# Channel attention: extremes of keys by a chain of maxima, one row of exponentials added on VectorE, inverses by logarithm and one Newton step

## The chip, the cores and the metric

The kernel runs on one core of a Trainium2 chip, as one program. The time is the core's own, in microseconds; three runs were made of the kernel before. One more execution was profiled.

## The reference

Four layers act on x of shape (4, 256, 64, 64) in float32, each as x + layer(group_norm(x)): a windowed attention, a linear attention, a channel attention over 7 x 7 windows, and a dynamic convolution. The change touches the third:

```python
q = jnp.einsum('bchw,oc->bohw', x, w_q)
kmap = jnp.einsum('bchw,oc->bohw', x_pad, w_k)
vmap = jnp.einsum('bchw,oc->bohw', x_pad, w_v)
...
kwin = jnp.concatenate([kwin[:, :half] + rel_h, kwin[:, half:] + rel_w], axis=1)
...
attn = jax.nn.softmax(q[..., None] * kwin, axis=-1)
out = jnp.sum(attn * vwin, axis=-1)
```

Each channel of each pixel has a softmax of its own over its 49 neighbours: the score is q times (key + bias), where the bias depends on the window's row in the first 128 channels and on its column in the other 128. So per pixel and channel there are 49 exponentials, a sum of them, a sum of them times the values, and one division.

## The kernel before

The function `channel_attention` works on bands of 16 image rows (`NB` = 16 of them, 4 images x 4). A band has four tiles of 128 channels x 512 pixels (8 rows): half h (channels) = 0, 0, 1, 1 and part u = 0, 1, 0, 1. Below, a tile with u = 0 is called even, with u = 1 odd. There are 64 tiles in all. A tile has 49 steps j, one for each tap: seven rows o of seven taps i. All five engines walk through (band, tile, step) in their own loops, written out for one band and repeated by a hardware loop; what stands in which step is set by small tables of step numbers (`PROJ_AT`, `NEAR`, `EXT_AT`, `INVERT_AT`, `DIVIDE_AT`, `BACK_AT`, `ADD_AT`), and semaphores with counts join the engines.

A step of each engine:

- VectorE, `multiply` (L1795): (key + bias) x query into one of three banks of PSUM, `stage`. It waits until the exponential three steps back has read that bank.
- TensorE, `shift` (L1545): a product with minus the identity takes from the same bank the largest score `top`. Then `add_up` (L1552): four transposes of 128 x 128 add the map of exponentials of two steps back to `pe_sum`, and four more the weighted map of twelve steps back to `pv_sum`. The order in a step is weighted map, shift, exponentials.
- ScalarE, `exponential` (L1671): the exponential of the bank into `se`, which has four buffers of seven taps each (a row).
- GpSimd, `weigh` (L1705): four or three taps of exponentials times the values, into `ev`. Two of these make a row of seven, 14 a tile.

Beside that, in the tables' steps:

- The largest score is found ahead, for the half that comes next. `near_step_of` (VectorE) takes the maximum and the minimum over four keys, along a row of the image or down a column, depending on the half: L1742 makes that of two neighbours (`pair`), and L1752, a `tensor_reduce` over a pattern of 2 x 2 elements of `pair` at distances 3 and 2, makes that of seven in a row (`near`). Keys come in four parts, `near` in two pieces for each part and extreme: 8 pairs and 16 reductions for a half, all in steps 4 to 33 of the even tile. `extreme_step` then goes over the seven windows (L1769, L1771) and multiplies by the query (L1778, L1780): 34 operations for a half, 10 in the even tile from step 34 on and 24 in the odd one. Below they are called extremes.
- `project` (TensorE, L1534) makes the next half's keys, queries and values in the bank `pj`, in ten parts of two steps each; ScalarE copies each part out (L1645), two steps after it was begun. Before the next part may be written the bank has to be copied. Even tiles have six parts (keys and queries), odd ones four (values).
- The division of tile t-1 falls into tile t: ScalarE copies `pe_sum` to `es` in step 1 (L1659, `take_e_sums`), VectorE inverts it in four pieces in steps 3, 5, 7 and 9 (L1803), multiplies in step 12 (L1811), TensorE turns the result back in step 20 and VectorE adds it to x in step 23 (L1819).

The buffers `se` are freed for the row four rows later by two conditions: summed on TensorE and weighed on GpSimd.

## Time and profile before

| | us |
|---|---|
| median of 3 runs | 9316.44 (9316.26 to 9318.12) |
| profiled execution | 9307.04 |
| its span | 9305.5 |
| TensorE busy | 8011.6 (86%) |
| VectorE busy | 5823.2 (63%) |
| ScalarE busy | 3539.4 (38%) |
| GpSimd busy | 4537.8 (49%) |

The channel attention runs from about 4,040 to 8,210 us of the span. PE is TensorE (PEld its weight loads), DVE VectorE, ACT ScalarE and POOL GpSimd. The digits of a slice are tenths of its time in which the engine was busy. Durations of two instructions that follow each other overlap a little, so the time that one takes from a queue is read from the distance of two starts. In brackets at the end of a timeline's row stands the idle time before it, and what ended it.

### The profile page before, as it was taken

The numbers are of one execution on the slowest core, as the hardware profiler recorded it, in microseconds if no ns is written. First come the engines' busy times: TensorE is split into PE (matmuls) and PEld (weight loads), VectorE is DVE, ScalarE is ACT, GpSimd is POOL, SyncE is SP. The second block draws the span as 40 slices with busy tenths as digits, with TensorE's granted clock in tenths as the row PEclk, the third lists the DMA queues.
The fourth block names the chain that finished last, engine by engine and source line by source line (L and its number), as shares of the span: only waits on it lengthen the run. The fifth ranks groups of instructions, "written<-read, shape, count | busy, mean of one in ns | idle before, by whom it ended". The sixth has DMA issues, their size and how long they took to land. (4 is left out here: it accounts for less than half of the span.)

```text
span 9305.5 us, 159969 instructions
## 1 busy us (share of the span) xinstructions
PE 8011.6 (86%) x55850; PEld 6805.6 (73%) x55850; DVE 5823.2 (63%) x9258; ACT 3539.4 (38%) x6969; POOL 4537.8 (49%) x2070
## 2 busy tenths in 40 slices
PE   3888886759996777569999999999999999938999
PEld 2666664649996565458888888888888888836777
DVE  3555555454442343479888989888888889842110
ACT  3444444313332222234445545444445545530000
POOL 2444443003332000047778878777777878831111
PEclk9999998879998888889999999999999999969999
DMA  5111113846775455410000000000000000052111
GB/s 195 52 52 61 53 52 129 295 143 144 146 146 142 173 160 149 159 70 17 6 17 17 17 17 17 17 13 17 6 17 17 17 17 17 8 164 105 63 61 55
DMA packets 435343, 703.76 MB, mean 76 GB/s; under 512 B 273645, under 2 KB 280301, under 8 KB 425390
## 3 DMA queue, kind: packets, MB, share of 16 engines
q1 hardware_dynamic: 389550, 502.28, 17.4%
q0 software_dynamic: 38656, 176.79, 6.3%
q10 hardware_dynamic: 6528, 16.78, 0.6%
q8 instruction: 357, 5.85, 0.3%
q14 instruction: 252, 2.06, 0.1%
HBM read 422.53 MB, written 273.22 MB: 75 GB/s over the span
## 5 line engine op out<-in xcount | busy, mean ns | idle before, releaser
L1705 POOL TENSOR_TENSOR e_ev<-e_se,e_v 128x2048 f32<-128x2048 f32 (+1 forms) x896 | 3311.6, 3714 | 916.6 <-ACT e_se L1671 916.6
L1671 ACT ACTIVATE e_se<-e_stage 128x512 f32<-128x512 f32 x3136 | 1878.2, 599 | 2082.4 <-PE e_stage L1545 2056.3
L1795 DVE SCALAR_TENSOR_TENSOR e_stage<-e_k,e_rl,e_qp 128x512 f32<-128x512 f32 x3136 | 2302.6, 746 | 318.6 <-ACT e_se L1671 279.2
L1552 PE MATMUL e_pv_sum<-e_ident,e_ev 128*128 128x128 f32 x12544 | 1874.1, 273 | 38.1 <-issue 37.6
L1552 PE MATMUL e_pe_sum<-e_ident,e_se 128*128 128x128 f32 x12544 | 1878.0, 272 | 0.1
L1552 PEld LDWEIGHTS e_pe_sum<-e_ident,e_se 128*128 128x128 f32 x12544 | 1556.3, 139 | 227.3 <-issue 2.0
L1552 PEld LDWEIGHTS e_pv_sum<-e_ident,e_ev 128*128 128x128 f32 x12544 | 1487.9, 141 | 264.8 <-issue 211.4
L1545 PE MATMUL e_stage<-e_top,e_minus 128*128 128x512 f32 x3136 | 1508.7, 481 | 45.3 <-DVE e_stage L1795 43.9
L363 POOL TENSOR_TENSOR a_pr<-a_pr,a_rden 128x480 f32<-128x480 f32 x512 | 493.9, 985 | 683.0 <-DVE a_rden L583 683.0
L852 POOL DMA_DIRECT2D agg<-c_ot x384 | 329.0, 862 | 950.9 <-DVE c_ot L910 839.1
L886 PE MATMUL c_pa<-c_x_high,c_w_high 128*128 128x320 f32 x1920 | 602.3, 314 | 111.4 <-DVE c_w_low L965 111.4
L1545 PEld LDWEIGHTS e_stage<-e_top,e_minus 128*128 128x128 f32 x3136 | 596.1, 190 | 98.3 <-DVE e_stage L1795 71.4
L1534 PE MATMUL e_pj<-e_xb,e_wt 128*128 128x385 f32 (+5 forms) x1280 | 572.8, 531 | 72.6 <-ACT e_v L1645 60.9
L548 ACT ACTIVATE a_pr<-a_ps,a_nmax 128x240 f32<-128x240 f32 x1024 | 459.0, 461 | 402.8 <-DVE a_nmax L577 402.8
L886 PE MATMUL c_pa<-c_x_high,c_w_low 128*128 128x320 f32 x1920 | 603.8, 315 | 0.0
L886 PE MATMUL c_pa<-c_x_low,c_w_high 128*128 128x320 f32 x1920 | 602.1, 314 | 0.0
L1771 DVE SCALAR_TENSOR_TENSOR e_ext<-e_near,e_rl,e_ext 128x512 f32<-128x512 f32 x768 | 575.3, 749 | 0.9
L577 DVE TENSOR_REDUCE a_nmax<-a_ps 128x2 f32<-128x480 f32 x512 | 312.1, 651 | 406.9 <-PE a_ps L441 406.9
L1752 DVE TENSOR_REDUCE e_near<-e_pair 128x192 f32<-128x768 f32 (+2 forms) x512 | 514.7, 1005 | 0.6
L2100 DVE TENSOR_TENSOR f_xr<-f_pc,f_xr 128x512 f32<-128x512 f32 x64 | 44.2, 691 | 742.6 <-PE f_pc L2013 742.6
L1967 POOL TENSOR_TENSOR f_x_low<-f_xb,f_x_high 128x1400 fp32r<-128x1400 f32 x32 | 106.3, 3326 | 796.6 <-ACT f_x_high L2043 796.6
L2013 PE MATMUL f_pc<-f_x_high,f_w_high 128*128 128x512 f32 x1152 | 467.3, 406 | 22.3 <-POOL f_x_low L1967 22.3
(154 smaller groups left out, 12357.7 us busy)
## 6 DMA issues: line engine op xcount, KB each, us to landing
xn<-n_xnp POOLq DMA_DIRECT2D x32, 2450.0 KB, 14.9
qkv<-b_ot SPq DMA_DIRECT2D x120, 512.0 KB, 5.8
c_xt<-qkv SPq DMA_DIRECT2D x384, 160.0 KB, 4.3
agg<-c_ot POOLq DMA_DIRECT2D x384, 160.0 KB, 3.0
n_xt<-x SPq DMA_DIRECT2D x24, 2048.0 KB, 11.8
a_xb<-xn SPq DMA_DIRECT2D x32, 840.0 KB, 6.2
e_xb<-xn SPq DMA_DIRECT2D x16, 1540.0 KB, 7.0
f_xb<-xn SPq DMA_DIRECT2D x32, 700.0 KB, 6.0
```

The costliest lines, as they stand in the source:

```text
L363: nc.gpsimd.tensor_tensor(w, w, by, ALU.mult).then_inc(normalised, 1)
L548: last = nc.scalar.activation(pr[P % BUF][:, i, e, :], ps[:, 2 * s + i, e * NK:(e + 1) * NK], ACT.Exp, bias=nmax[P % BUF][:, i, e:e + 1], ...
L886: last = nc.tensor.matmul(pa[:, u, b, 0:NBLK * WW].rearrange("p (k c) -> p k c", c=WW), lhsT=w[u][:, dx].rearrange("p o y -> p (o y)"), rh ...
L1534: last = nc.tensor.matmul(out, lhsT=wt[:, w, g, (h % 2) * PART:(h % 2 + 1) * PART], rhs=rhs, start=g == 0, stop=g == HALVES - 1)
L1545: nc.tensor.matmul(stage[:, bank_of(t, j), :], lhsT=minus[:], rhs=top[h][:, u * TPX:(u + 1) * TPX], start=False, stop=True, skip_group_che ...
L1552: last = nc.tensor.matmul(acc[:, c * PART:(c + 1) * PART], lhsT=src[:, c * PART:(c + 1) * PART], rhs=ident[:], is_transpose=True, start=j ...
L1671: nc.scalar.activation(se[(t * K2 + o) % NSE][:, i], stage[:, bank_of(t, j), :], ACT.Exp)\
L1705: nc.gpsimd.tensor_tensor(split(ev[(t * NG2 + g) % NEV][:, 0:size]), split(se[(t * K2 + o) % NSE][:, i:i + size]), window(v[h], h, u, o, i ...
L1752: nc.vector.tensor_reduce(to, pairs, AX.XY, op).then_inc(near_step, 1)
L1771: nc.vector.scalar_tensor_tensor(rows(ext[:]), win, r[:, o:o + 1], rows(ext[:]), ALU.add, op)\
L1795: nc.vector.scalar_tensor_tensor(rows(stage[:, bank_of(t, j), :]), win, rl[:, h, o:o + 1], rows(qp[:]), ALU.add, ALU.mult).then_inc(multip ...
L2013: last = nc.tensor.matmul(pc[:, u, m].rearrange("p (r c) -> p r c", c=WW), lhsT=w[:, g, t, m * PART:(m + 1) * PART], rhs=x[:, g, dy:dy + R ...
```

## The change

Four things are changed, all in `channel_attention`.

The extreme of seven keys is made by three elementwise operations instead of two: of two neighbours (`pair`, as before), of four (`four`, a buffer of one part), and of seven, written back into `pair`. The 2 x 2 reductions and the buffer `near` are gone; the number and the steps of the pieces stay.

The seven exponential maps of window row 3 (`SUM_ROW`) are no longer added on TensorE one by one. VectorE adds them in four pieces of 128 pixels, in steps 31, 33, 35 and 37 of the same tile, into `row_sum`, and TensorE adds that once, in step 41. Each piece is a `tensor_reduce` over seven elements that lie 512 elements (2 KB) apart.

The inverse of the sum of exponentials is no longer VectorE's reciprocal. ScalarE makes exp(-ln(es)) in step 3, GpSimd multiplies it by the sum (`check`, after its second weighing), and VectorE makes (product - 2) x estimate in step 10, which is minus the inverse after one Newton step. The addition to x becomes a subtraction.

Of the extremes, which `EXT_AT` spreads over free steps, some move by one to four steps, since other steps are free now.

```diff
-        near = [sb(f"near{i}", [PART, HPX]) for i in range(2)]
+        four = [sb(f"four{i}", [PART, 6 * PW]) for i in range(2)]
...
+        row_sum = sb("row_sum", [PART, TPX])
...
-        INVERT_AT = (3, 5, 7, 9)
-        NINV = len(INVERT_AT)
-        DIVIDE_AT, BACK_AT, ADD_AT = 12, 20, 23
+        SUM_ROW = 3
+        ROW_AT = (31, 33, 35, 37)
+        NROW = len(ROW_AT)
+        ROW_ADD_AT = 41
+        NSUM = NTAP - K2 + 1
+        LN_AT, CHECK_AFTER = 3, 1
+        INVERT_AT, DIVIDE_AT, BACK_AT, ADD_AT = 10, 12, 20, 23
...
-            + [(1, j) for j in range(NTAP - 2) if j not in (*INVERT_AT, DIVIDE_AT, ADD_AT)]
+            + [(1, j) for j in range(NTAP - 2) if j not in (INVERT_AT, DIVIDE_AT, ADD_AT, *ROW_AT)]
...
             def sum_exponential(n, t, j, first=False):
                 o, i = divmod(j, K2)
+                if o == SUM_ROW:
+                    return
...
+            def sum_row(n, t):
+                pe.wait_ge(row_summed, tiles(n, t, NROW, NROW))
+                add_up(pe_sum, row_sum, SUM_ROW * K2).then_inc(e_summed, 1)
...
+                if j == ROW_ADD_AT:
+                    sum_row(n, t)
...
+            def nearly_invert(n, t):
+                act.wait_ge(e_taken, tiles(n, t, 1, 1))
+                if later(n, t):
+
+                    act.wait_ge(divided, tiles(n, t, 1, 0))
+                nc.scalar.activation(rs[:], es[:], ACT.Ln).then_inc(near_inverse, 1)
+                act.wait_ge(near_inverse, tiles(n, t, 2, 1))
+                nc.scalar.activation(rs[:], rs[:], ACT.Exp, scale=-1.0).then_inc(near_inverse, 1)
...
+                if j == LN_AT and (t or not first):
+                    nearly_invert(n, t - 1)
...
+            def check(n, t):
+
+                pool.wait_ge(near_inverse, tiles(n, t, 2, 2))
+                nc.gpsimd.tensor_tensor(es[:], es[:], rs[:], ALU.mult).then_inc(checked, 1)
...
-                pairs = bass.AP(tensor=a.tensor, offset=a.offset,
-                                ap=[a.ap[0], [PW, tall], [1, wide], [3 * away, 2], [2 * away, 2]])
...
-                nc.vector.tensor_reduce(to, pairs, AX.XY, op).then_inc(near_step, 1)
+                high_, wide = (size, PW) if h % 2 == 0 else (HR, size)
+                of_four = four[i][:, 0:high_ * wide].rearrange("p (r c) -> p r c", c=wide)
+                if piece == 1:
+
+                    src, to, by, count_ = key_part(pair[i][:], h, c), of_four, 2, (PW, HR)[h % 2] - 3
+                else:
+                    src, to, by, count_ = of_four, key_part(pair[i][:], h, c), 3, (WW, R2)[h % 2]
...
+                nc.vector.tensor_tensor(to, a, z, op).then_inc(near_step, 1)
...
-            def invert(n, t, p):
+            def sum_row(n, t, p):
...
+                nc.vector.tensor_reduce(row_sum[:, s], se[(t * K2 + SUM_ROW) % NSE][:, :, s].rearrange("p i x -> p x i"),
+                                        AX.X, ALU.add).then_inc(row_summed, 1)
+
+            def invert(n, t):
+
+                dve.wait_ge(checked, tiles(n, t, 1, 1))
+                nc.vector.scalar_tensor_tensor(rs[:], es[:], 2.0, rs[:], ALU.subtract, ALU.mult).then_inc(inverted, 1)
```

How the order moves, at three places of the first band, which is written out. In a row stands the line, the operation, what it writes and reads, and how many follow each other. First ScalarE in the second tile (odd), from the copy of the sums on; e_se is an exponential, e_v a copy of projected values. Before:

```order
L1659 ACTIVATE e_es<-e_pe_sum 128x512
L1671 ACTIVATE e_se<-e_stage 128x512
L1645 ACTIVATE e_v<-e_pj 128x385
L1671 ACTIVATE e_se<-e_stage 128x512 x2
L1645 ACTIVATE e_v<-e_pj 128x385
```

and now:

```order
L1685 ACTIVATE e_es<-e_pe_sum 128x512
L1706 ACTIVATE e_se<-e_stage 128x512
L1671 ACTIVATE e_v<-e_pj 128x385
L1706 ACTIVATE e_se<-e_stage 128x512
L1692 ACT_TABLE_LOAD
L1692 ACTIVATE e_rs<-e_es 128x512
L1694 ACT_TABLE_LOAD
L1694 ACTIVATE e_rs<-e_rs 128x512
L1706 ACTIVATE e_se<-e_stage 128x512
L1671 ACTIVATE e_v<-e_pj 128x385
```

Between the exponentials of steps 3 and 4 stand two table loads and two activations, in this tile as in every other.

Second, VectorE in steps 31 to 38 of the same tile; e_stage is a multiply, e_ext an extreme. Before:

```order
L1795 SCALAR_TENSOR_TENSOR e_stage<-e_k,e_rl,e_qp 128x512 x2
L1769 TENSOR_SCALAR e_ext<-e_near,e_rl 128x512
L1795 SCALAR_TENSOR_TENSOR e_stage<-e_k,e_rl,e_qp 128x512
L1771 SCALAR_TENSOR_TENSOR e_ext<-e_near,e_rl,e_ext 128x512
L1795 SCALAR_TENSOR_TENSOR e_stage<-e_k,e_rl,e_qp 128x512 x2
```

and now:

```order
L1844 SCALAR_TENSOR_TENSOR e_stage<-e_k,e_rl,e_qp 128x512
L1855 TENSOR_REDUCE e_row_sum<-e_se 128x128
L1844 SCALAR_TENSOR_TENSOR e_stage<-e_k,e_rl,e_qp 128x512
L1820 SCALAR_TENSOR_TENSOR e_ext<-e_pair,e_rl,e_ext 128x512
L1844 SCALAR_TENSOR_TENSOR e_stage<-e_k,e_rl,e_qp 128x512
L1855 TENSOR_REDUCE e_row_sum<-e_se 128x128
L1844 SCALAR_TENSOR_TENSOR e_stage<-e_k,e_rl,e_qp 128x512 x2
L1855 TENSOR_REDUCE e_row_sum<-e_se 128x128
L1844 SCALAR_TENSOR_TENSOR e_stage<-e_k,e_rl,e_qp 128x512
L1820 SCALAR_TENSOR_TENSOR e_ext<-e_pair,e_rl,e_ext 128x512
L1844 SCALAR_TENSOR_TENSOR e_stage<-e_k,e_rl,e_qp 128x512
L1855 TENSOR_REDUCE e_row_sum<-e_se 128x128
```

Each of the four reductions stands behind a multiply and ahead of the next.

Third, TensorE at the start of row 3, in step 22 and after it in the first tile; e_pj is a projection. Now:

```order
L1563 MATMUL e_stage<-e_top,e_minus 128x512
L1570 MATMUL e_pe_sum<-e_ident,e_se 128x128 x4
L1570 MATMUL e_pv_sum<-e_ident,e_ev 128x128 x4
L1563 MATMUL e_stage<-e_top,e_minus 128x512
L1570 MATMUL e_pv_sum<-e_ident,e_ev 128x128 x4
L1563 MATMUL e_stage<-e_top,e_minus 128x512
L1552 MATMUL e_pj<-e_xb,e_wt 128x374
```

The row e_pe_sum is missing from the second step on, for seven steps; before, it stands in each.

## Rows read from the trace of the kernel before

**Rows 1.** The page: busy tenths of its 40 slices

```profile
PE   3888886759996777569999999999999999938999
DVE  3555555454442343479888989888888889842110
```

**Rows 2.** Busy times by tile, an even, an odd and an even tile

```profile
core 0: us, PE busy (x) PEld busy (x) DVE busy (x) ACT busy (x) POOL busy (x), PEclk, DMA share, GB/s
6009.30:6073.90 64.60, 64.32 (x470) 55.20 (x469) 60.53 (x90) 32.75 (x58) 51.62 (x15) 1.00 0.05 18
6073.90:6137.00 63.10, 60.66 (x461) 53.66 (x459) 52.58 (x78) 32.00 (x56) 52.27 (x15) 1.00 0.01 2
6137.00:6208.00 71.00, 67.40 (x468) 56.26 (x469) 65.25 (x91) 32.48 (x57) 50.87 (x15) 0.98 0.01 2
```

**Rows 3.** Waits of 2,000 us of the stage: us in total, times, longest

```profile
DVE e_stage L1795 <- ACT e_se L1671: 129.0, 213, 2.4
```

**Rows 4.** Timeline of a steady step (start us, us, engine, line)

```profile
6000.48 0.48 PE L1545 MATMUL e_stage<-e_top,e_minus 128*128 128x512 f32 x1
6000.79 0.60 PE L1552 MATMUL e_pe_sum<-e_ident,e_se 128*128 128x128 f32 x4
...
6000.99 0.60 ACT L1671 ACTIVATE e_se<-e_stage 128x512 f32<-128x512 f32 x1 [0.51 <-PE e_stage L1545]
...
6001.23 0.60 PE L1552 MATMUL e_pv_sum<-e_ident,e_ev 128*128 128x128 f32 x4
6001.58 0.48 PE L1545 MATMUL e_stage<-e_top,e_minus 128*128 128x512 f32 x1
```

**Rows 5.** Timeline of an even tile: TensorE late, VectorE without a gap

```profile
6025.48 0.50 PE L1545 MATMUL e_stage<-e_top,e_minus 128*128 128x512 f32 x1 [0.22 <-DVE e_stage L1795]
...
6027.09 0.75 DVE L1795 SCALAR_TENSOR_TENSOR e_stage<-e_k,e_rl,e_qp 128x512 f32<-128x512 f32 x1
6027.74 0.95 DVE L1752 TENSOR_REDUCE e_near<-e_pair 128x192 f32<-128x768 f32 x1
6028.60 0.74 DVE L1795 SCALAR_TENSOR_TENSOR e_stage<-e_k,e_rl,e_qp 128x512 f32<-128x512 f32 x1
```

**Rows 6.** Timeline of TensorE, projections in an odd tile

```profile
6074.81 0.81 PE L1534 MATMUL e_pj<-e_xb,e_wt 128*128 128x385 f32 x2
6075.46 0.60 PE L1552 MATMUL e_pv_sum<-e_ident,e_ev 128*128 128x128 f32 x4
...
6079.13 0.92 PE L1534 MATMUL e_pj<-e_xb,e_wt 128*128 128x385 f32 x2 [0.63 <-ACT e_v L1645]
```

**Rows 7.** Timeline of TensorE at a band's turn

```profile
6139.00 0.63 PE L1552 MATMUL e_pv_sum<-e_ident,e_ev 128*128 128x128 f32 x4 [2.54 <-issue]
```

**Rows 8.** The reductions L1752: by form, then one of each kind with 512 elements

```profile
L1752 DVE TENSOR_REDUCE e_near<-e_pair 128x144 f32<-128x576 f32 x192 | 222.8, 1161 | 0.0
L1752 DVE TENSOR_REDUCE e_near<-e_pair 128x192 f32<-128x768 f32 x192 | 181.2, 944 | 0.4
...
6039.02 0.68 DVE L1752 TENSOR_REDUCE e_near<-e_pair 128x128 f32<-128x512 f32 x1
...
6172.54 1.04 DVE L1752 TENSOR_REDUCE e_near<-e_pair 128x128 f32<-128x512 f32 x1
```

**Rows 9.** Groups by form, VectorE and GpSimd

```profile
L1803 DVE RECIPROCAL e_rs<-e_es 128x128 f32<-128x128 f32 x256 | 242.0, 946 | 119.2 <-ACT e_es L1659 119.2
...
L1742 DVE TENSOR_TENSOR e_pair<-e_pj,e_k 128x345 f32<-128x345 f32 x64 | 32.7, 511 | 2.0
...
L1705 POOL TENSOR_TENSOR e_ev<-e_se,e_v 128x2048 f32<-128x2048 f32 x448 | 1890.8, 4220 | 810.4 <-ACT e_se L1671 810.4
L1705 POOL TENSOR_TENSOR e_ev<-e_se,e_v 128x1536 f32<-128x1536 f32 x448 | 1437.0, 3208 | 106.2 <-ACT e_se L1671 106.2
```

**Rows 10.** Timeline of ScalarE at a table load, first stage

```profile
24.64 3.86 ACT L150 ACTIVATE n_xnp<-n_xt,n_coef 128x4096 f32<-128x4096 f32 x1 [0.48 <-DVE n_coef L127]
28.52 1.28 ACT L145 ACT_TABLE_LOAD   x1
```

More of the change, by code:

```diff
@@ L1449, in bank_lag, with later, adds @@
             return 2 if t * NTAP + j in (1, TPB * NTAP - 1) else NST
+        def later(n, t):
+            return not isinstance(n, int) or n * TPB + t > 0
+        def adds(j):
+            if j // K2 == SUM_ROW:
+                return adds(ROW_ADD_AT - E_LAG - 1) + 1
+            return j + 1 - (K2 if j // K2 > SUM_ROW else 0) + (j >= ROW_ADD_AT - E_LAG)
         def group_of(j):
@@ L1654, in take_e_sums @@
             def take_e_sums(n, t):
[L1655 to L1658 removed]
+                act.wait_ge(e_summed, tiles(n, t, NSUM, NSUM))
+                if later(n, t):
+                    act.wait_ge(inverted, tiles(n, t, 1, 0))
                 nc.scalar.activation(es[:], pe_sum[:], ACT.Copy).then_inc(e_taken, 1)
+            def nearly_invert(n, t):
+                act.wait_ge(e_taken, tiles(n, t, 1, 1))
+                if later(n, t):
+                    act.wait_ge(divided, tiles(n, t, 1, 0))
+                nc.scalar.activation(rs[:], es[:], ACT.Ln).then_inc(near_inverse, 1)
+                act.wait_ge(near_inverse, tiles(n, t, 2, 1))
+                nc.scalar.activation(rs[:], rs[:], ACT.Exp, scale=-1.0).then_inc(near_inverse, 1)
             def exponential(n, t, j, first=False):
@@ L1667, in exponential @@
                     t0, j0 = before(t, j, NSE * K2)
-                    act.wait_ge(e_summed, tiles(n, t0, NTAP, j0 + size))
+                    act.wait_ge(e_summed, tiles(n, t0, NSUM, adds(j0 + size - 1)))
                     act.wait_ge(weighted, tiles(n, t0, NG2, group_of(j0) + 1))
@@ L1712, in band @@
                         weigh(n, t, g, first)
+                        if g == CHECK_AFTER and (t or not first):
+                            check(n, t - 1)
             band(0, first=True)
@@ L1716, in _ @@
                 band(n)
+            check(NB - 1, TPB - 1)
         @block.vector
@@ L1743, in near_step_of @@
                     return
-                part = size // 2
-                low, part = (first, part) if piece == 1 else (first + part, size - part)
-                at, tall, wide = (low * PW, part, WW) if h % 2 == 0 else (low, R2, part)
-                a = pair[i][:, at:at + 1]
-                pairs = bass.AP(tensor=a.tensor, offset=a.offset,
-                                ap=[a.ap[0], [PW, tall], [1, wide], [3 * away, 2], [2 * away, 2]])
-                a = near[i][:, at:at + 1]
-                to = bass.AP(tensor=a.tensor, offset=a.offset, ap=[a.ap[0], [PW, tall], [1, wide]])
-                nc.vector.tensor_reduce(to, pairs, AX.XY, op).then_inc(near_step, 1)
+                high_, wide = (size, PW) if h % 2 == 0 else (HR, size)
[4 more added lines that the diff above has]
+                    src, to, by, count_ = of_four, key_part(pair[i][:], h, c), 3, (WW, R2)[h % 2]
+                if h % 2 == 0:
+                    to, a, z = to[:, :, 0:count_], src[:, :, 0:count_], src[:, :, by:by + count_]
+                else:
+                    to, a, z = to[:, 0:count_, :], src[:, 0:count_, :], src[:, by:by + count_, :]
+                nc.vector.tensor_tensor(to, a, z, op).then_inc(near_step, 1)
             def extreme_step(n, h, s):
@@ L1766, in extreme_step @@
                 if o < K2:
-                    win = one_window(near[i], w * RT * PW + (o * PW if h % 2 == 0 else o))
+                    win = one_window(pair[i], w * RT * PW + (o * PW if h % 2 == 0 else o))
                     if o == 0:
@@ L1842, in _ @@
             all_bands(dve, step)
-            for p in range(NINV):
-                invert(NB - 1, TPB - 1, p)
+            invert(NB - 1, TPB - 1)
             divide(NB - 1, TPB - 1)
```

27 lines of the change are left out of this document (15 added, 12 removed).

## The prediction

> **What bounds the kernel now.** I read the page first: of its 40 slices the 18 from about 4,000 to 8,200 us are the channel attention, the only stage that the diff touches, and in them TensorE stands at 9 tenths with VectorE at 8 or 9 [rows 1]. Then the busy times of three consecutive tiles [rows 2]. An odd tile (u=1) takes 63.1 us with TensorE busy for 60.7 and VectorE for 52.6. An even tile (u=0), which also holds the extremes' first steps, takes 64.6 us with VectorE busy for 60.5, and at a band's start 71.0 with VectorE at 65.3. The stage has 16 bands of some 261 us, two tiles of each kind. The table of waits shows VectorE waiting for an exponential to free its bank, 129 us in 2,000, so at those times it is ahead [rows 3].
>
> A steady step of TensorE [rows 4]: from one shift (L1545) to the next 1.10 us, of which four transposes that add one exponential map take 0.44 (start of the e_pe_sum row to start of the e_pv_sum row). An exponential follows its shift's start by 0.51 us and takes 0.60. With three stage banks multiply j needs exponential j-3, so VectorE can be ahead by at most 3 x 1.11 less 1.11 (shift and exponential) less 0.75 (the multiply) = 1.4 us. That lead is all the cover there is. In even tiles TensorE already waits for VectorE [rows 5]: 49 steps of 1.107 are 54.2 us, the projections add about 8.5 (twelve products of 350 to 512 columns, 0.58 to 0.85 each by columns, from the 0.65 between the starts of a 385-column product and of what follows it [rows 6]), turning back 0.4, so 63.2. The tile has 64.6: 1.4 us late; the other even tile, less some 5 us of its band's turn (TensorE stands for 2.54 us with nothing to wait for [rows 7], and two slow steps follow), 2.6 late.
>
> **The change, part by part.** Tile means one of 64.
>
> (1) TensorE drops seven groups of four transposes and gains one, the sum of row 3: 6 x 0.44 = 2.65 us a tile, 170 us in all. This is the gain, if TensorE is fed.
>
> (2) It isn't fed in steps 23 to 29, where a step shrinks to 0.66 us. A multiply occupies VectorE for 0.66 (starts 6027.09 and 6027.74 [rows 5]), an extreme of the second kind as much. In an odd tile these steps hold 7 multiplies, three extremes and one addition: 7.2 us, less a lead of 1.0 = 6.2, where TensorE could do 4.66. Of the 3.1 us that go from these steps 1.55 come. In an even tile TensorE has a projection there (5.8 us) and VectorE 6.8 less 1.3: all 3.1 come. So (2) costs 1.55 in odd tiles.
>
> (3) The row sums: four reductions of 896 elements to 128. The trace has no reduction with a step of 2 KB between the seven. It has two kinds of L1752 [rows 8]: pairs along a row (steps of 2 or 3 elements) take 0.94 us for 768 elements and 0.68 for 512, that is 1.04 ns an element; pairs down a column (steps of 560 and 840 bytes) take 1.16 for 576 and 1.04 for 512, that is 1.84. Bounds: 1.07 and 1.75 us. I take 1.75, since here too each element lies far from the last; on VectorE's queue it counts 0.09 less, 1.66. In steps 30 to 37 of an odd tile VectorE then has 8 multiplies, three extremes and four reductions: 7.26 + 6.64 = 13.9 us, with no lead left, against TensorE's 8 x 1.107 = 8.86: 5.0 us lost. In an even tile: 8 multiplies, three extremes, four short pieces of the chain (0.42 each) are 9.0, + 6.64 = 15.6, against 8.86 + 3.4 of projections and 0.3 of lead: 3.0 lost. The pieces stand at steps 31, 33, 35 and 37; at 31, 33 and 35 of an even tile a chain step or an extreme follows in the same step.
> Beside the row: the Trainium skill (SBUF — State Buffer, Door 1: The DMA port swizzle, the note on cachelines) says that an access which crosses to another 16-byte line pays a penalty. That holds of a 2 KB step as of the column pairs, and by it (3) is the 1.75; without it the 1.07. The trace agrees as far as 840 bytes.
>
> (4) What VectorE is spared. Four reciprocals of 0.87 (0.95 less the overlap [rows 9]) become one of 0.66: 2.8 us a tile, in steps 3 to 10. Sixteen reductions per half become sixteen elementwise maxima of 272 to 402 elements: by the elementwise row (345 elements, 0.51 us [rows 9]) and 1.04 ns an element 0.35 to 0.5 each, 5.6 us saved in one kind of half, 10.6 in the other. In even tiles this takes away the lateness: 2.0 us on the mean of 1.4 and 2.6. In odd tiles TensorE wasn't waiting there: nothing. No operation of VectorE in this stage has both inputs in SBUF; the maxima and the new inverse have, beside a busy GpSimd. I price that at nothing; the other end is that each takes twice as long, 16 x 0.45 = 7 us in an even tile (rival D).
>
> (5) ScalarE gets two table loads, a logarithm and an exponential between exponential 3 and 4 of each tile, as the order shows. A load is 1.28 us and started when the activation before it ended (28.52 [rows 10]); 1.28 + 0.60 + 1.28 + 0.60 is 3.7 us of a queue in which the next exponentials stand. From shift 3: exponential 3 ends at 1.1, exponential 4 at 5.4. TensorE wants it at step 6, at 3.5: 1.9 us lost in an even tile. In an odd tile step 4 projects into the bank that ScalarE copies out after exponential 4; today TensorE waits 0.63 to 0.9 us there [rows 6], and gets the bank 2.55 us later. No row shows a ready activation directly behind a load: the other end is rival C.
>
> (6) GpSimd's product, about 1.2 us (the slope between its two forms [rows 9]), stands behind its second weighing; it is busy for 52 of 63 us, so that costs nothing itself. VectorE's inverse at step 10 waits for it until about 11 us after shift 3 in an even tile and 14.5 in an odd one, while multiply 11 is wanted a microsecond later: nothing lost, but the lead starts again from near zero. I used that in (2).
>
> Sum. Odd tile: -2.65 + 1.55 + 5.0 + 2.55 = +6.45; 32 of them, +206. Even tile: -2.65 + 3.0 + 1.9 - 2.0 = +0.25; +8. The start of the stage has 16 cheaper maxima (-6), its end the new inverse's chain (+2). +210 on the profiled 9307.0 gives 9517; the median of the runs is 9.4 above it, so **9526 us**.
>
> **The rivals.** (B) The reduction runs at 1.04 ns an element. Then (3) costs 7.26 + 3.92 - 8.86 = 2.3 in odd tiles and about 0.2 in even ones, the sum is 32 x 3.75 - 32 x 2.55 = +38: 9355. For it: the row pairs; against it: the column pairs. (A) Faster: ScalarE's block at step 3 isn't seen, because a load between two functions of one table set costs nothing or the exponentials behind it are covered. That takes (5) away, 64 x 2.2 = 142 us. With the dear reduction the kernel is still slower by 68; with the cheap one it comes to 9213. It decides from a block under 1.8 us (3.7 less what an even tile covers). The built program has both loads, which speaks against it. The Trainium skill (ScalarE: Activation LUTs, Table sets: the hidden batching unit) speaks for one load where a set with both functions is used; the order shows two. (C) A load holds ScalarE for longer than its row. If each held it as long again as its own row, 64 x 2.6 = 164 us more: 9690. For it: nothing in the rows, against it nothing either. The skill (the same page, What ACT_TABLE_LOAD costs) counts 2.66 us for a switch with its drain; by that figure the sum would be 9702. (D) VectorE and GpSimd hinder each other in the chain of maxima: 32 tiles x 6 us more, 9715. (E) The change doesn't do what it says, TensorE isn't relieved: it does, the order has 24 transposes fewer in a tile.
>
> **How the numbers follow.** Forecast as summed, 0.57; B 0.14; A 0.08; C 0.15; D 0.06. The forecast's own uncertainty (lead, steps) is about 80 us to either side. The range takes in B, C and the forecast and leaves out A and most of D: 9340 to 9710. A measurement of this kernel can tell about 0.2%, 19 us, from no change. Faster by more: A, 0.08. Within: the lower edge of B, 0.04. Slower: 0.88.
>
> **What would show it.** Right: in tiles' windows the odd tile near 69 to 70 us and the even near 65; TensorE's busy time in the stage down while the tile grows; the reduction of e_se at 1.7 us; VectorE without a gap through steps 30 to 38 and TensorE's shifts waiting for it; a gap of some 3.7 us between exponentials 3 and 4, with both loads in it. Wrong: a reduction of 1.07 us (B), exponential 4 within 2 us (A), loads followed by idle time (C), maxima of L1801 near a microsecond (D). A granted TensorE clock under 1.00 in the stage's middle (it is 1.00 in two of the three tiles, 0.98 in the one with the turn [rows 2]) would add to all of them.

## The result, and the profile after

The changed kernel takes 10081.8 us (median of 4 runs, 10068.0 to 10090.7), the one before 9316.4: 1.082 times as long (95% interval 1.080 to 1.084). The prediction had 9526 and a range up to 9710. The direction was right, the size was not: 765 us and not 210.

The page of the changed kernel, busy tenths by slice and the granted clock, answers to [rows 1]:

```profile
PE   4888884789977774888888888888888888855999
DVE  4555554454433344888888888888888888853110
PEclk9999997889988887999999999999999999977999
```

The stage now fills 20 slices, and in them TensorE is at 8 tenths and not at 9. The busy times of one band by tile (even, odd, even at the band's turn, odd) answer to [rows 2]:

```profile
core 0: us, PE busy (x) PEld busy (x) DVE busy (x) ACT busy (x) POOL busy (x), PEclk, DMA share, GB/s
6052.22:6134.68 82.46, 68.80 (x448) 56.63 (x446) 73.47 (x90) 36.11 (x63) 53.89 (x16) 0.94 0.04 14
6134.68:6206.37 71.69, 63.20 (x447) 53.63 (x445) 57.85 (x81) 35.71 (x60) 53.88 (x16) 0.98 0.00 1
6206.37:6292.14 85.77, 70.49 (x440) 57.21 (x439) 72.85 (x90) 35.97 (x61) 52.69 (x16) 0.90 0.01 2
6292.14:6362.91 70.77, 62.27 (x440) 52.80 (x438) 57.85 (x81) 35.63 (x61) 52.90 (x16) 0.98 0.12 38
```

Even tiles take 82.5 and 85.8 us where they took 64.6 and 71.0; odd ones 71.7 and 70.8 where they took 63.1 and 62.5. So of some 49 us a band, two thirds lie in the even tiles, which the prediction had almost unchanged. (These and all tile times below are of one band; in other bands the same tile can differ by up to 3 us.) VectorE's busy time in an even tile went up from 60.5 to 73.5 us, though by the prices of the prediction it was given less work. In the table of waits TensorE's wait for VectorE, which was 13.8 us before, is 200.6 us in 2,000:

```profile
PE e_stage L1563 <- DVE e_stage L1844: 200.6, 191, 4.2
```

What VectorE does in that time shows in the timeline of an even tile. First GpSimd, then VectorE (start us, us, engine, line):

```profile
6083.68 7.66 POOL L1743 TENSOR_TENSOR e_ev<-e_se,e_v 128x2048 f32<-128x2048 f32 x2 [3.50 <-ACT e_se L1706]
...
6085.62 2.70 DVE L1801 TENSOR_TENSOR e_four<-e_pair 128x402 f32<-128x402 f32 x1
6088.24 0.74 DVE L1844 SCALAR_TENSOR_TENSOR e_stage<-e_k,e_rl,e_qp 128x512 f32<-128x512 f32 x1
6088.89 2.86 DVE L1801 TENSOR_TENSOR e_pair<-e_four 128x384 f32<-128x384 f32 x1
...
6092.34 0.49 DVE L1801 TENSOR_TENSOR e_four<-e_pair 128x335 f32<-128x335 f32 x1
```

GpSimd's first weighing of this pair starts at 6083.68 and, being 4.2 us long, ends at 6087.9. The maximum of 402 elements that starts at 6085.62 ends at 6088.32. The second weighing ends at 6091.34; the maximum started at 6088.89 ends at 6091.75. Then GpSimd is idle until 6097.40, and the next maximum, of 335 elements, takes 0.49 us. The sixteen maxima of this tile take 23.6 us together, where by their size they would take 8. Both their inputs lie in SBUF; the maxima of two neighbours, with one input in PSUM, take 0.50 to 0.59 us as before, in whatever state GpSimd is.

The tile is no exception. Of the 512 maxima with two SBUF inputs in the whole stage, 290 started while GpSimd was idle and took 0.42 to 0.58 us, each by its size. 222 started while GpSimd worked; 221 of them ended 0.30 to 0.44 us after the end of the GpSimd instruction that was under way.

The row sums and ScalarE's block, in the same views. The reductions by form:

```profile
L1855 DVE TENSOR_REDUCE e_row_sum<-e_se 128x128 f32<-128x896 f32 x104 | 180.2, 1733 | 0.0
```

ScalarE from exponential 3 to exponential 4 of an odd tile, and the projection of TensorE that waits for the copy behind it:

```profile
6143.67 0.60 ACT L1706 ACTIVATE e_se<-e_stage 128x512 f32<-128x512 f32 x1 [1.67 <-PE e_stage L1563]
6144.29 1.28 ACT L1692 ACT_TABLE_LOAD   x1
6145.58 0.63 ACT L1692 ACTIVATE e_rs<-e_es 128x512 f32<-128x512 f32 x1
6146.23 1.28 ACT L1694 ACT_TABLE_LOAD   x1
6147.52 0.63 ACT L1694 ACTIVATE e_rs<-e_rs 128x512 f32<-128x512 f32 x1
6148.06 0.58 ACT L1706 ACTIVATE e_se<-e_stage 128x512 f32<-128x512 f32 x1
...
6149.07 1.00 PE L1552 MATMUL e_pj<-e_xb,e_wt 128*128 128x385 f32 x2 [3.24 <-ACT e_v L1671]
```

Each load is 1.28 us and the activation behind it starts as it ends. From the end of exponential 3 to the start of exponential 4 there are 3.8 us. TensorE stands for 3.24 us, and behind that its granted clock (the number behind the five busy times) is 0.69, then 0.50, the lower of its two levels, and in the third stretch, some four microseconds later, 0.95:

```profile
6149.00:6151.00 2.00, 1.93 (x7) 1.54 (x8) 1.08 (x2) 0.02 (x1) 0.00 (x0) 0.69 0.00 0
6151.00:6153.00 2.00, 2.00 (x7) 1.41 (x6) 0.76 (x1) 0.60 (x1) 0.00 (x0) 0.50 0.03 8
6153.00:6155.00 2.00, 1.51 (x10) 0.96 (x8) 0.26 (x1) 0.89 (x2) 0.21 (x1) 0.95 0.00 0
```

The fall of the clock is frequent behind this stop, but it isn't bound to it. The same stop of 3.24 or 3.25 us stands in all 31 odd tiles that have a projection in step 4. In 28 of them the clock falls, in 3 it does not, as here, five odd tiles earlier (a row of the timeline, then two stretches with the granted clock at the same place as above):

```profile
5376.56 0.91 PE L1552 MATMUL e_pj<-e_xb,e_wt 128*128 128x385 f32 x2 [3.25 <-ACT e_v L1671]
...
5376.56:5378.56 2.00, 2.00 (x12) 1.61 (x13) 1.02 (x2) 0.37 (x1) 0.00 (x0) 1.00 0.00 0
5378.56:5380.56 2.00, 1.78 (x12) 1.16 (x10) 0.76 (x1) 0.84 (x3) 0.00 (x0) 1.00 0.00 0
```

From the distances of the shifts, steps 4 to 6 of an odd tile take 2.6 us longer than before where the clock stays, and 4.2 to 4.3 where it falls (5.3 in two tiles). What decides between the two stays open.

### The profile page after: what moved, and what is told of

It is laid out like the page before. It is cut to its first block and busy times, and to the rows that moved or that the text cites. A ratio compares the mean times of both kernels' runs of the same rounds, so it can differ in the third digit from the quotient of the medians.

```text
span 10079.7 us, 158198 instructions
## 1 busy us (share of the span) xinstructions
PE 8171.4 (81%) x54314; PEld 6801.3 (67%) x54314; DVE 6300.8 (63%) x9322; ACT 3765.5 (37%) x7225; POOL 4640.0 (46%) x2134
## 5 line engine op out<-in xcount | busy, mean ns | idle before, releaser
L1563 PE MATMUL e_stage<-e_top,e_minus 128*128 128x512 f32 x3136 | 1573.6, 502 | 520.9 <-DVE e_stage L1844 515.9
L1570 PE MATMUL e_pv_sum<-e_ident,e_ev 128*128 128x128 f32 x12544 | 1938.8, 280 | 35.1 <-issue 34.7
L1570 PEld LDWEIGHTS e_pv_sum<-e_ident,e_ev 128*128 128x128 f32 x12544 | 1557.4, 145 | 327.3 <-issue 256.0
L1570 PE MATMUL e_pe_sum<-e_ident,e_se 128*128 128x128 f32 x10752 | 1664.5, 278 | 56.0 <-ACT e_se L1706 55.9
L1570 PEld LDWEIGHTS e_pe_sum<-e_ident,e_se 128*128 128x128 f32 x10752 | 1370.7, 143 | 265.8 <-ACT e_se L1706 65.7
L1563 PEld LDWEIGHTS e_stage<-e_top,e_minus 128*128 128x128 f32 x3136 | 619.1, 197 | 682.2 <-DVE e_stage L1844 660.7
L1552 PE MATMUL e_pj<-e_xb,e_wt 128*128 128x385 f32 (+5 forms) x1280 | 621.5, 571 | 151.0 <-ACT e_v L1671 141.6
L1820 DVE SCALAR_TENSOR_TENSOR e_ext<-e_pair,e_rl,e_ext 128x512 f32<-128x512 f32 x768 | 576.4, 751 | 0.9
L2072 PE MATMUL f_pc<-f_x_low,f_w_high 128*128 128x512 f32 x1152 | 466.4, 405 | 0.0
```

The source lines that it names most:

```text
L1552: last = nc.tensor.matmul(out, lhsT=wt[:, w, g, (h % 2) * PART:(h % 2 + 1) * PART], rhs=rhs, start=g == 0, stop=g == HALVES - 1)
L1563: nc.tensor.matmul(stage[:, bank_of(t, j), :], lhsT=minus[:], rhs=top[h][:, u * TPX:(u + 1) * TPX], start=False, stop=True, skip_group_che ...
L1570: last = nc.tensor.matmul(acc[:, c * PART:(c + 1) * PART], lhsT=src[:, c * PART:(c + 1) * PART], rhs=ident[:], is_transpose=True, start=j ...
L1820: nc.vector.scalar_tensor_tensor(rows(ext[:]), win, r[:, o:o + 1], rows(ext[:]), ALU.add, op)\
L2072: last = nc.tensor.matmul(pc[:, u, m].rearrange("p (r c) -> p r c", c=WW), lhsT=w[:, g, t, m * PART:(m + 1) * PART], rhs=x[:, g, dy:dy + R ...
```

## The experiments

Theory 1: a VectorE operation with two inputs in SBUF, started while GpSimd works, is held until GpSimd is through; the even tiles' loss is that. Theory 2: the loads block ScalarE for their rows' length and not longer, and the stop costs a second time where TensorE's clock falls behind it. Theory 3: the row sums are dear by the distance of their inputs and by where they stand. The rivals stand in the texts below. Even tiles of a band come in two kinds, in the middle and at the turn; both are given, as middle / turn.

### The three parts, each alone

Only the chain of maxima on the kernel before (`chain_alone`); the edit is the change's own, without the rest:

```diff
-                nc.vector.tensor_reduce(to, pairs, AX.XY, op).then_inc(near_step, 1)
...
+                nc.vector.tensor_tensor(to, a, z, op).then_inc(near_step, 1)
```

> The kernel before with the chain of maxima alone (16 elementwise maxima a half, both inputs in SBUF, in place of 16 reductions); row sums and inverses as before. Theory 1 (VectorE's operation with two inputs in SBUF is held until GpSimd's instruction under way has ended): in the changed kernel eight or nine of the sixteen took 1.2 to 4.2 us and the others 0.45 to 0.55, 17 us more than their own work in an even tile. Here the same: even tiles 8 to 15 us longer, odd tiles unchanged at 63, in all 9570 to 9800. Rival 1 (the even tiles' loss comes from the row sums and ScalarE's block, and the long maxima only fill time in which VectorE would wait anyway): even tiles lose their lateness, 2 us each, 9240 to 9320.

Measured: 9604.9 us, 1.032 (1.030 to 1.033). By tile, an odd one and the even one in the middle:

```profile
6087.33:6149.89 62.56, 60.66 (x463) 53.91 (x462) 54.63 (x80) 31.88 (x56) 51.69 (x15) 1.00 0.13 43
6149.89:6224.88 74.99, 67.10 (x472) 56.80 (x470) 69.44 (x89) 32.88 (x58) 52.48 (x15) 0.98 0.05 15
```

Even tiles 75.0 / 79.5, odd tiles 62.6 and 63.5, as before. Theory 1 stands; the chain alone costs 288 us.

Only the inverse by logarithm and exponential (`inverse_alone`), which leaves `nearly_invert`, `check` and `invert` of the change and nothing else.

> The kernel before with the inverse by logarithm, exponential and Newton step alone. By the prediction's step 5: 1.9 us lost in an even tile, 2.55 in an odd one, less about a microsecond of reciprocals in even tiles: 32 x 2.55 + 32 x 0.9 = 110, 9430. Theory 2 adds that TensorE, after standing for 3.2 us, runs at half its clock for some 4 us, as in the changed kernel (granted clock 0.69 and 0.50 in the two stretches behind the stop): 1.3 us more in odd tiles, 9470. Rival (a load holds ScalarE for longer than its row): 9600 or more.

Measured: 9538.3 us, 1.024 (1.023 to 1.026), 222 us. An odd tile and an even one:

```profile
6043.01:6109.40 66.39, 61.88 (x462) 54.62 (x461) 52.16 (x77) 35.53 (x60) 52.77 (x16) 0.97 0.13 41
6109.40:6177.31 67.91, 65.10 (x474) 55.51 (x471) 57.57 (x85) 36.42 (x62) 53.21 (x16) 1.00 0.05 17
```

Odd tiles 66.0 and 66.4, 3 us longer; even tiles 67.9 / 74.0, also 3 us longer, where 0.9 was expected. A load that holds ScalarE for longer is out. The size was off by 70 us. By the shifts, an even tile loses 1.96 us at step 6, which waits for exponential 4, and another 1.0 at step 10, where the inverse stands. In the odd tiles the clock fell behind the stop in 18 of 31, and those lost 4.0 to 5.6 us in steps 4 to 6; in the other 13 it stayed, and they lost 2.6.

Only the row sums (`row_alone`): `SUM_ROW`, `ROW_AT` and `ROW_ADD_AT` of the change.

> The kernel before with row 3 added on VectorE alone. By the prediction's steps 1 to 3: odd tiles -2.65 + 1.55 + 5.0 = +3.9 us. Even tiles have the reductions of the extremes as before and are full already, so that 6.6 us more of VectorE less what TensorE gives up gives 3 to 6 us: 9540 to 9630. Rival (VectorE's slack takes the row sums, and TensorE's 2.65 us are gained): 9150 to 9250.

Measured: 9605.6 us, 1.031 (1.029 to 1.033), 289 us. An odd and an even tile:

```profile
6091.38:6157.69 66.31, 60.15 (x436) 51.14 (x434) 59.94 (x83) 31.81 (x55) 51.10 (x15) 1.00 0.13 41
6157.69:6227.32 69.63, 65.02 (x452) 53.57 (x450) 66.56 (x93) 33.01 (x59) 52.30 (x15) 1.00 0.05 16
```

Odd tiles 66.3 and 67.1 against 62.6 and 63.5, 3.7 us longer; even tiles 69.6 / 77.1, 5 to 6 us longer. The shifts tell where an even tile in the middle loses. In steps 23 to 29, where TensorE has 3.1 us less to do, they are 8.4 us apart in all and were 9.1: VectorE works without a gap there, and 0.75 us comes of the 3.1. Steps 30 to 37 take 16.8 us and took 12.4. The three parts cost 288 + 222 + 289 = 799 us, the whole change 765.

The whole change without the chain (`no_chain`):

> The changed kernel with the extremes by reductions as before, so without any maximum with two inputs in SBUF. Theory 1: odd tiles stay at 71, even tiles fall from 84 to 73 to 76; 9700 to 9830. Rival 1 (the chain isn't what costs): no faster than the changed kernel, 10080, or slower by the 8 us of VectorE that the chain was to save a half.

Measured: 9822.0 us, 1.055 (1.053 to 1.056), 506 us, where inverse and row sums alone add up to 511. Even tiles 72.1 / 79.6, odd 70.0 and 71.9.

### What holds a maximum

GpSimd's weighing in one instruction for each tap in place of three and four (`chain_short_pool`, on `chain_alone`):

```diff
-                nc.gpsimd.tensor_tensor(split(ev[(t * NG2 + g) % NEV][:, 0:size]),
-                                        split(se[(t * K2 + o) % NSE][:, i:i + size]),
-                                        window(v[h], h, u, o, i, size), ALU.mult).then_inc(weighted, 1)
+                for e in range(size):
+                    last = nc.gpsimd.tensor_tensor(rows_of(ev[(t * NG2 + g) % NEV][:, e]),
+                                                   rows_of(se[(t * K2 + o) % NSE][:, i + e]),
+                                                   window(v[h], h, u, o, i + e, 1)[:, 0], ALU.mult)
+                last.then_inc(weighted, 1)
```

> chain_alone with GpSimd's weighing cut into one instruction for each tap, so about 1.2 us each in place of 3.2 and 4.2, the same work. Theory 1 (a VectorE operation with two SBUF inputs is held until the GpSimd instruction under way ends): no maximum of the chain takes over 1.8 us, where the longest took 3.8; their mean falls from 1.2 to 0.7 to 1.0; even tiles fall from 77 to 68 to 72; in all 9390 to 9500. Rival 1a (the two engines slow each other for as long as both run, by a shared rate): the mean of the maxima and the time stay, 9600.

Measured: 9272.1 us, 0.996 (0.995 to 0.997): faster than expected, and than the kernel before. The maxima in this kernel (shortest, median and longest in ns):

```profile
L1757 DVE TENSOR_TENSOR e_four<-e_pair x256: 508/827/1528, 4003.4 to 7950.6; 128x402 f32<-128x402 f32 x32, 128x335 f32<-128x335 f32 x32, 128x342 f32<-128x342 f32 x32, 128x323 f32<-128x323 f32 x32
L1757 DVE TENSOR_TENSOR e_pair<-e_four x256: 486/790/1276, 4004.0 to 7952.0; 128x384 f32<-128x384 f32 x32, 128x320 f32<-128x320 f32 x32, 128x288 f32<-128x288 f32 x32, 128x272 f32<-128x272 f32 x32
```

None takes over 1.53 us, where 3.84 was the longest. Even tiles 64.5 / 69.3, odd ones as before. A rate shared between two working engines is out as the cause, since GpSimd does the same work for longer. That the median is 0.8 us and not 0.5 is the same hold with shorter pieces: 496 of the 512 maxima started beside a working GpSimd, and every one of them ended 0.29 to 0.44 us after the end of its instruction; the 16 others took 0.49 to 0.58. The sixteen of a tile take 13.3 us in the mean, where the reductions before took some 14 and 18 by half, so most of what the chain was to save isn't saved even here.

The same cut without the chain (`short_alone`):

> The kernel before with GpSimd's weighing cut into one instruction a tap and nothing else. Theory 1: VectorE has no operation with two SBUF inputs here, so nothing is held and GpSimd, busy for 57 of 63 us a tile, stays off the path: 9300 to 9330, the same as before; the gain of chain_short_pool, 46 us, is then the chain's, from the even tiles' lateness (the prediction's 2.0 us a tile would be 66). Rival (shorter GpSimd instructions free buffers earlier and gain by themselves): 9270 to 9290.

Measured: 9315.4 us against 9309.3, 1.0005 (0.9997 to 1.0014). So the gain of `chain_short_pool` is the chain's.

The whole change with the cut (`after_short`):

> The changed kernel with GpSimd's weighing cut into one instruction a tap. If the three parts add up (chain with short pieces -46, inverse +222, row sums +289), 9780; theory 1 allows 9700 to 9800, since the even tiles have more room for the row sums when the chain is short: even tiles 72 to 75, odd ones 71. Rival (the parts' costs overlap, the slowest alone decides): under 9650.

Measured: 9782.2 us, 1.051 (1.050 to 1.053). Even tiles 73.0 / 76.1. The cut takes 300 us off the changed kernel; what remains is the inverse and the row sums. The even tile still takes 8.4 us more than in `chain_short_pool`, so the cheaper chain gives the row sums no room: steps 23 to 29 take 8.2 us, and VectorE has no gap in them.

### What the loads cost

`inverse_alone` with a copy where the logarithm stood (it leaves out the logarithm and so computes no inverse, and no load is needed):

```diff
-                nc.scalar.activation(rs[:], es[:], ACT.Ln).then_inc(near_inverse, 1)
+                nc.scalar.activation(rs[:], es[:], ACT.Copy).then_inc(near_inverse, 1)
```

> inverse_alone with a copy in the place of the logarithm, which leaves the inverse wrong and needs no table load; all instructions, waits and buffers else are the same. Theory 2 (the block of ScalarE's queue costs, and the stop of TensorE behind it lowers its clock): the block shrinks from 3.7 to 1.1 us, odd tiles lose at most 0.5 us and no clock, 9330 to 9380, that is 160 to 200 less than with loads. Rival (GpSimd's product and VectorE's wait for it cost, not the loads): within 60 us of 9538.

Measured: 9394.1 us, 1.008 (1.006 to 1.010): 144 us less than with loads. Odd tiles are back at 62.4 and 63.3; even ones, at 66.8 / 72.7, are still 2 us longer than before. So the loads with their clock are the whole loss of the odd tiles, and two thirds of the inverse's cost. The rest lies in even tiles. VectorE waits for GpSimd's product in step 10, 70 us in 2,000:

```profile
6062.32 0.69 DVE L1833 SCALAR_TENSOR_TENSOR e_rs<-e_es,e_rs 128x512 f32<-128x512 f32 x1 [3.41 <-POOL e_es L1736]
```

TensorE's shift behind it comes 2.93 us after the one before, where it came after 1.11: 1.8 of the two microseconds in the middle tile. No run takes this wait away by itself.

### What makes the row sums dear

`row_alone` with each reduction reading 896 neighbouring elements in groups of seven (it leaves out the sum over the row's seven maps):

```diff
-                nc.vector.tensor_reduce(row_sum[:, s], se[(t * K2 + SUM_ROW) % NSE][:, :, s].rearrange("p i x -> p x i"),
+                nc.vector.tensor_reduce(row_sum[:, s], se[(t * K2 + SUM_ROW) % NSE][:].rearrange("p i x -> p (i x)")[:, p * (K2 * TPX // NROW):(p + 1) * (K2 * TPX // NROW)].rearrange("p (x i) -> p x i", i=K2),
```

> row_alone with each reduction reading 896 elements that lie side by side, in groups of seven, in place of seven 2 KB apart; the row's sum is wrong by that. Theory 3 (the price is the distance): a reduction takes 1.07 us and not 1.73, 2.6 us of VectorE less in a tile; odd tiles fall from 66.7 to 64.0 to 64.5, even ones by 2 to 2.6; in all 9430 to 9460. Rival (the reductions stand in the way whatever they take, for want of lead): above 9550.

Measured: 9451.9 us, 1.014 (1.012 to 1.016), 154 us less than `row_alone`. The reduction (shortest, median, longest in ns):

```profile
L1833 DVE TENSOR_REDUCE e_row_sum<-e_se x256: 1066/1082/1222, 4112.3 to 8330.6; 128x128 f32<-128x896 f32 x128
```

It takes 1.08 us, where the bound from [rows 8] was 1.07, and odd tiles 63.7 and 64.5. In `row_alone` its median was 1.75, so the distance of the inputs is 0.67 us of each piece. But even the cheap reductions left the kernel slower than before, so their placing was tried.

Row 3 on VectorE in odd tiles alone, on `chain_short_pool` (`row_in_odd`). The tables, set against those of the change; the addition to x moves from step 23 to 22, and the counts of sums now differ between tiles:

```diff
-        ROW_AT = (31, 33, 35, 37)
+        ROW_AT = (30, 34, 38, 42)
-        ROW_ADD_AT = 41
+        ROW_ADD_AT = 46
...
+        EXT_AT = [(0, j) for j in (34, 35, 37, 38, 40, 42, 43, 45, 47, 48)] \
+            + [(1, j) for j in (0, 0, 1, 1, 2, 2, 3, 4, 4, 5, 6, 6, 7, 8, 10, 11, 13, 15, 16, 18, 20, 43, 45, 46)]
```

> chain_short_pool with row 3 added on VectorE in odd tiles alone, its four pieces in steps 30, 34, 38 and 42, no extreme in steps 21 to 42 of those tiles (they are packed into steps 0 to 20, where TensorE has projections, and 43 to 46), the sum taken in step 46, the addition to x in step 22. Four reductions of 1.66 us and 20 multiplies of 0.66 in steps 23 to 42 are 19.8 us, with 1.4 us of lead, against 19.1 of TensorE. If density is what made the row sums dear, odd tiles fall from 63.0 to 60.3 to 61.5: 9190 to 9240. Rival (a reduction of 1.7 us between two multiplies always stops TensorE): 9290 or more.

Measured: 9328.9 us against 9309.3, 1.003 (1.002 to 1.004). Odd tiles 62.3 and 61.9, a microsecond better; the even tile in the middle went from 64.5 to 69.5. TensorE's shifts around step 30 of an odd tile:

```profile
6095.63 0.48 PE L1569 MATMUL e_stage<-e_top,e_minus 128*128 128x512 f32 x1
6096.31 0.48 PE L1569 MATMUL e_stage<-e_top,e_minus 128*128 128x512 f32 x1
...
6098.57 0.50 PE L1569 MATMUL e_stage<-e_top,e_minus 128*128 128x512 f32 x1 [0.91 <-DVE e_stage L1832]
...
6099.70 0.48 PE L1569 MATMUL e_stage<-e_top,e_minus 128*128 128x512 f32 x1
```

The fast steps are 0.67 us apart: VectorE keeps up when it has nothing but multiplies. The first reduction behind them stops TensorE, 2.26 us in place of 1.11. The even tile's 5 us are one maximum, held for 4.98 us: step 8 takes 5.1 us where it took 1.81.

The pieces in steps 33, 37, 41 and 45, the sum in step 47, the extremes all in steps 0 to 21 of odd tiles, up to three in a step (`row_odd_late`), and the same on the kernel before, without chain and cut (`row_odd_plain`):

> row_in_odd with the four pieces in steps 33, 37, 41 and 45, the row's sum in step 47, and no extreme behind step 21 of odd tiles. In row_in_odd TensorE's steps 23 to 29 took 0.67 us each, and step 30, with the first piece, 2.26: while steps are short VectorE can be ahead by 3 x 0.67 - 1.86 = 0.15 us alone, so a piece right behind them stops TensorE for 1.2 us. With three free steps ahead of each piece the stop goes: odd tiles 60.5 to 61.2 where they took 62.1, that is 30 to 50 us. The even tiles are as before; what the long hold of one maximum there (4.98 us) does is open: 9240 to 9300. Rival (a piece stops TensorE wherever it stands): odd tiles 62 and 9320.

Measured: 9388.4 us, 1.009 (1.007 to 1.010).

> The same placing on the kernel before: reductions for the extremes and GpSimd's weighing as before, no chain. Odd tiles 60.5 to 61.2 against 63.0 of before, even tiles as before, 64.8 and 71: 9316 less 32 x 1.8 to 2.5 = 9235 to 9260. If it is faster than row_odd_late by 30 us or more, the long holds of single maxima cost more than the cheaper extremes bring when VectorE's operations shift against GpSimd's.

Measured: 9289.9 us against 9310.3, 0.998 (0.997 to 0.999). In both, steps 23 to 46 of the odd tile run at 0.67 and 1.11 us: the four reductions, 1.78 us each, cost nothing. Odd tiles were 62.9 and 62.2 all the same, since three extremes in a step made steps 0 to 6 longer by 1.9 us and steps 7 to 13 by 0.45. And in `row_odd_late` the even tile in the middle took 72.2, with this maximum in it (GpSimd first, then VectorE):

```profile
6020.81 19.57 POOL L1738 TENSOR_TENSOR e_ev<-e_se,e_v 128x512 f32<-128x512 f32 x17
...
6034.48 6.33 DVE L1789 TENSOR_TENSOR e_four<-e_pair 128x402 f32<-128x402 f32 x1
```

GpSimd works off 17 pieces without a pause until 6040.38, and the maximum is held through the one under way and five more, to 6040.81. So a hold can outlast the instruction under way. In `row_in_odd`, `row_odd_late` and `row_odd_chain` 17 to 20 of the 512 maxima were held for 4.2 to 6.4 us. All were the first of the sixteen of their tile, and all ended 0.37 to 0.44 us after the last GpSimd instruction ahead of a pause. Others start in such a run and take 0.8 to 1.0 us. What tells them apart stays open, and whether GpSimd's instructions with one input hold a maximum too was not tried.

At most two extremes in a step of the odd tile and two more of them in the even one, and the addition to x in step 23 of even tiles again, on `row_odd_plain` (`row_odd_two`) and on `row_odd_late` (`row_odd_chain`):

```diff
-        DIVIDE_AT, BACK_AT, ADD_AT = 12, 20, 22
+        DIVIDE_AT, BACK_AT, ADD_AT = 12, 20, (23, 22)
...
-            + [(1, j) for j in (0, 0, 0, 1, 1, 2, 2, 2, 3, 4, 4, 4, 5, 6, 6, 6, 8, 10, 13, 14, 16, 18, 19, 21)]
+            + [(1, j) for j in (0, 0, 1, 1, 2, 2, 3, 4, 4, 5, 6, 6, 7, 8, 10, 13, 14, 16, 17, 19, 20, 21)]
```

> row_odd_plain with at most two extremes in a step of the odd tile (22 in steps 0 to 21, 12 in the even tile) and the addition to x back in step 23 of even tiles. In row_odd_plain TensorE's steps 23 to 47 of an odd tile were without a stop (0.67, then 1.11 us), the row sums cost nothing there, and the tile lost 2.4 us in steps 0 to 6, where three extremes stood in a step, and 0.9 us in step 22 of the even tile, where the addition met a reduction. Odd tiles 60.3 to 60.9, even tiles 64.7 and 71.0: 9310 less 32 x 2.1 to 2.7 = 9225 to 9245, faster than the kernel before and than chain_short_pool. Rival (the extremes have no free place left in any step): 9280 or more.

Measured: 9245.6 us against 9317.0, 0.992 (0.990 to 0.993), the fastest version. Its tiles (even at the turn, odd, even, odd):

```profile
6110.71:6182.50 71.79, 67.90 (x474) 56.83 (x473) 64.69 (x91) 33.01 (x58) 52.98 (x15) 0.98 0.01 2
6182.50:6242.21 59.71, 57.70 (x432) 50.51 (x429) 59.23 (x82) 31.79 (x55) 49.55 (x14) 1.00 0.14 45
6242.21:6308.00 65.79, 65.50 (x480) 56.31 (x479) 61.08 (x91) 32.90 (x57) 53.75 (x16) 1.00 0.05 17
6308.00:6368.49 60.49, 58.48 (x437) 51.20 (x435) 59.33 (x82) 31.83 (x56) 50.32 (x15) 1.00 0.00 1
```

These windows are cut close to VectorE's first multiply of a tile, and with them odd tiles are 2.8 to 3.0 us shorter and the even one in the middle a microsecond longer. TensorE's shifts show that this microsecond belongs to the odd tile: steps 23 to 48 of the odd tile are 2.6 us shorter than before, TensorE's 2.65 in full, but its steps 0 to 15, into which the extremes were packed, are 0.8 us longer; every step of the even tile in the middle takes what it took. By the shifts odd tiles are 1.8 and 2.1 us shorter and the even tile at the turn 0.9; in all the kernel gains 71 us.

> The same placing on row_odd_late (chain of maxima, GpSimd's weighing by taps). If the holds were as in chain_short_pool, 40 us less than row_odd_two, 9190. But in row_odd_late the first maximum of each fourth tile was held for 6.3 us, until a run of 17 GpSimd instructions was over, and in row_in_odd for 5.0. GpSimd is busy for 57 to 63 us a tile there and tiles get shorter: I expect the hold again, 5 us in 16 tiles and more: 9240 to 9330, slower than row_odd_two.

Measured: 9322.7 us, 1.000 (0.999 to 1.001). The same odd tiles, even tiles 71.7 / 68.3, the longest maximum 6.4 us.

### Other steps alone

The reductions and extremes of the kernel before in other steps, and nothing else (`spread_extremes`):

> The kernel before with other steps alone: the reductions of the extremes spread over steps 8 to 45 of the even tile (8 to 33 before) and the extremes moved out of it, 2 in the even tile and 32 in the odd. If the lateness of even tiles (1.4 and 2.6 us by the prediction's count) is VectorE's density in steps 3 to 33, they gain most of it, 30 to 60 us in all: 9255 to 9290. Rival (odd tiles have no room for eight more extremes, the same time or more comes back there): 9316 or above.

Measured: 9304.7 us against 9317.8, 0.999 (0.998 to 1.000). Even tiles 64.3 / 69.4, odd ones 64.0 and 63.2, where they were 64.8 / 71.0 and 63.5 and 62.6: most of what the even tiles gain comes back in the odd ones.

## Why the prediction was right or wrong

(1) Right as to what TensorE saves. With the placing of `row_odd_two` the 2.65 us come in the steps of odd tiles that it concerns; some 2.0 of them a tile are left in the kernel's time, since the extremes had to make room.

(2) and (3). In the odd tile: right. In the changed kernel steps 23 to 29 took 6.0 us (forecast 6.2) and steps 30 to 37 13.8 (forecast 13.9), the reduction 1.73 us (forecast 1.75); the row sums alone cost 3.7 us there (forecast 3.9). Wrong in one thought: the lead is a matter of the step's length, 3 steps less 1.86 us, so it falls to 0.15 us in the fast steps and isn't kept over them. It didn't change the sum, since the loss was counted in the steps behind. In even tiles: wrong, and a step that failed beside (4). The row sums alone cost 5 to 6 us there, and the forecast had 3.0 less 2.65, with the cheaper chain in place. It gave VectorE 5.5 us for steps 23 to 29 ("6.8 less 1.3" of lead) and so let all 3.1 us come. VectorE had no lead there and worked for 8.4 us without a gap (8.2 in `after_short`, with the cheaper chain); 0.75 to 1.0 us came (these and the next numbers are the middle tile's). Steps 30 to 37 lost 4.4 us (5.4 in `after_short`) for the 3.0. With the tile at the turn that is some 150 us in 32 tiles.

(4) The step that failed. It took the sixteen maxima in even tiles at 0.35 to 0.5 us each, "I price that at nothing" for two inputs in SBUF beside a busy GpSimd, and doubled them for rival D. Rival D had 7 us extra in a tile, and its sum 6. The maxima took 23.6 us where 8 is their own time, 15 to 16 us extra. The relief of 2.0 us became a loss of some 9 (`chain_alone`), 11 us in each of 32 tiles, 350 us or two thirds of the miss of 556. The mechanism was rival D's, with a price too low: not a slower rate but a hold for what is left of an instruction of 3.2 or 4.2 us. Those durations stood in [rows 9]; the other end of the bound should have been theirs. The Trainium skill has the rule (GPSIMD Engine Reference, 1. Specifications): GpSimd's SBUF interfaces are shared with VectorE, with contention when VectorE's instruction has two SBUF inputs. The trace agrees: beside a working GpSimd a maximum took up to 4.2 us, and with short pieces single ones took up to 6.4, where with GpSimd idle none took over 0.58.

(5) Mis-sized. The block is 3.8 us (forecast 3.7) and the even tile loses 1.96 us at step 6 (3.07 in place of 1.11 us; forecast 1.9). In the odd tile the projection gets its bank 2.6 us later, as forecast. In 28 of 31 odd tiles the clock then adds 1.6 to 1.7 us (2.7 in two of them): steps 4 and 5 took 8.7 us where they took 4.4. That is about 50 us in all. The prediction named the clock as something that would add, and gave it no price. Rival C fell: the activation starts as the load ends. The Trainium skill (ScalarE: Activation LUTs, What ACT_TABLE_LOAD costs) has 2.66 us for a switch with its drain; no part of that beyond the 1.28 shows in these rows.

(6) Wrong in even tiles. The forecast took GpSimd's product as free; without loads the inverse still costs these tiles 2 us, 1.8 of them at step 10, where VectorE waits for that product. With loads the step costs 1.0, some 30 us in 32 tiles.

The four pieces, 350 for the chain, 150 for the row sums in even tiles, 50 for the clock and 30 for step 10, are 580 us against a miss of 556. They overlap a little, as the parts alone do (799 against 765).

Rivals A and B: neither came. B's price was right (the reduction of neighbouring elements took 1.08 us), but the change doesn't read neighbours. D's 9715 is a slip: 32 times 6 us on 9526 is 9718.

Of the signs named, the odd tile near 70, the reduction at 1.7 us, the gap of 3.7 us and the maxima "near a microsecond" or above were to be read as they came; the even tile "near 65" was the sign against.

## What to carry to other kernels

Before giving VectorE an operation with two SBUF inputs, look at how long GpSimd's instructions are: the operation may wait for the rest of one, so keep one input in PSUM or cut GpSimd's work into short pieces. Work moved to an engine with spare time has to fit the lead, and the lead is set by the number of buffers times the length of a step: in odd tiles four reductions cost 5 us in steps 30 to 37, in every second step and with extremes between them, and nothing when three steps without any extreme stood ahead of each. A table switch in a queue that feeds the bounding engine costs the load, and the stop that it makes can cost again in TensorE's clock.
